# A graph layer on one core: 132 batches of gathered rows formed on TensorE in place of 128, and the node table laid out by 56 consecutive nodes to a partition

## The reference

```python
msg  = relu(x[src] + edge_attr @ We + be)
aggr = segment_sum(msg, dst, num_segments=6250)
h    = (1.0 + eps) * x + aggr
h    = relu(h @ W1 + b1) @ W2 + b2
h    = (h - mean(h, axis=0)) * rsqrt(var(h, axis=0) + 1e-5) * gamma + beta
out  = layernorm(x + relu(h) + x)
```

## Time and profile before

| | |
|---|---|
| median of 3 runs | 1557.24 us (1556.69 to 1558.63) |
| profiled execution, its own time | 1564.18 us |
| its span, first to last instruction | 1562.2 us |
| PE / PEld busy | 91% / 70% of the span |
| DVE / ACT / POOL busy | 57% / 80% / 74% |
| mean granted clock of TensorE | 0.981 |
| gathers of 128 rows | 31 out of x, 1145 out of xb, 3 for the last group |

### The profile page before, as it was taken

One profiled execution on the slowest core, in us unless ns is written; L12 is line 12 of the kernel. 1 busy time (PEld: TensorE's weight loads), 2 busy tenths in 40 slices (PEclk: granted clock), 3 DMA queues, 4 the chain that ended last, 5 costly groups with the idle time before them and its releaser, 6 DMA issues.

```text
span 1562.2 us, 60471 instructions
## 1 busy us (share of the span) xinstructions
PE 1416.0 (91%) x23435; PEld 1095.0 (70%) x23435; DVE 891.9 (57%) x3174; ACT 1255.7 (80%) x3729; POOL 1160.5 (74%) x1193
## 2 busy tenths in 40 slices
PE   1299999999999999989999999989999999999954
PEld 1277777777777777767777777767777777777734
DVE  5676665655566565555555556555556555655436
ACT  2488888888888888878877888878788888888845
POOL 7677777777777777777777777777777777777762
PEclk9999999999999999999999999999999999999967
DMA  9644445444544445444444444445444444444432
GB/s 250 170 111 109 109 113 123 113 111 117 119 113 110 108 112 126 109 106 113 111 108 106 113 106 113 112 106 117 108 110 107 111 112 107 105 112 110 104 125 84
DMA packets 148516, 180.72 MB, mean 116 GB/s; under 512 B 41725, under 2 KB 128980, under 8 KB 147972
## 3 DMA queue, kind: packets, MB, share of 16 engines
q1 hardware_dynamic: 102489, 89.62, 24.5%
q0 software_dynamic: 37728, 77.31, 20.9%
q10 hardware_dynamic: 8011, 9.90, 2.3%
HBM read 170.09 MB, written 6.63 MB: 113 GB/s over the span
## 4 chain that ended last, share of the span: by engine, by line
PE 55%; POOL 21%; issue 8%; ACT 5%; DVE 4%; DMA 4%; SPq 1%; ACTq 0%; POOLq 0%; DVEq 0%
POOL xg L590 21%; PE ps L1396 20%; PE ps L1381 14%; PE ps L1325 9%; PE ps L1311 6%; DMA xg<-xb,idxb 3%; ACT hot L747 2%; ACT msg L753 1%; PE ps L1362 1%; ACT hot L740 1%; PE ps L1342 1%; PE ps L1365 1%; PE ps L1334 1%; PE ps L1337 1%; SPq L480 1%
## 5 line engine op out<-in xcount | busy, mean ns | idle before, releaser
L590 POOL DMA_INDIRECT xg<-xb,idxb x1145 | 1107.0, 967 | 356.9 <-issue 337.0
L1396 PE MATMUL ps<-iota_all 128*128 128x128 bf16 x8064 | 518.0, 220 | 0.0
L1396 PEld LDWEIGHTS ps<-iota_all 128*128 128x128 bf16 x8064 | 452.3, 98 | 87.1 <-issue 67.7
L984 DVE TENSOR_TENSOR msg<-ps,xg 128x512 f32<-128x512 f32 x390 | 264.5, 688 | 305.6 <-DMA xg<-xb,idxb 192.8
L707 ACT ACTIVATE iota_all<-ps 128x384 bf16<-128x384 f32 x896 | 379.8, 484 | 31.7 <-PE ps L1381 28.4
L740 ACT ACTIVATE hot<-iota,rel 128x64 f32<-128x64 f32 x1560 | 391.6, 339 | 0.0
L1381 PE MATMUL ps<-x,iota_all 112*32 112x384 bf16 x7168 | 365.1, 331 | 0.0
L1069 DVE TENSOR_TENSOR accT<-accT,ps 128x64 f32 x390 | 86.2, 221 | 292.4 <-PE ps L1342 248.1
L753 ACT ACTIVATE msg<-msg 128x512 f32<-128x512 f32 x390 | 241.0, 618 | 14.7 <-DVE msg L984 14.7
L1381 PEld LDWEIGHTS ps<-x,iota_all 112*32 112x32 bf16 x7168 | 156.9, 96 | 120.6 <-issue 38.5
L1325 PE MATMUL ps<-msg,hot 128*64 128x128 f32 x3120 | 219.4, 284 | 23.1 <-ACT msg L753 23.1
(11 more groups left out here) (145 smaller groups left out, 800.3 us busy)
## 6 DMA issues: line engine op xcount, KB each, us to landing
ea<-in_eat SPq DMA_DIRECT2D x156, 320.0 KB
lowB<-lowD SPq DMA_DIRECT2D x128, 224.0 KB
xg<-xb,idxb POOLq DMA_INDIRECT x1145
accT<-in_xt ACTq DMA_DIRECT2D x1, 3125.0 KB, 14.8
x<-in_xt ACTq DMA_DIRECT2D x1, 3125.0 KB, 11.0
out<-iota_all SPq DMA_DIRECT2D x5, 512.0 KB
iota_all<-in_x ACTq DMA_DIRECT2D x3, 784.0 KB, 17.6
xb<-iota_all SPq DMA_DIRECT2D x3, 784.0 KB, 16.8
```

The lines of the kernel that those rows point to most:

```text
L590: pool.indirect_dma_start(out=xg[0:rows, slot, j, :], out_offset=None, in_=of, in_offset=bass.IndirectOffsetOnAxis(ap=index, axis=0)).then ...
L984: add = dve.tensor_tensor(both, lin_of(half), xg[:, g % RING, :, :].rearrange("p (b t) h -> p b (t h)", b=2), ALU.add)
L1396: last = pe.matmul(found[:, e, :], sel2[set_of(k)][:, t, e * P:(e + 1) * P], rows3[:, t, a, :], start=(t == 0 and e == 0 and a == 0), stop ...
```

## The change

* A batch's place in the loop is now computed: tile t of batch b is picked in visit (7b + t) * 90 // 217 - 3, and its group is three after the last of these. That is 31 batches in 90 groups where there were 30, with two or three tiles in every visit. The last batch is that of group 382, and there are 132 in all. With (7b + 6) * 90 // 217 the special groups up to 34 are 2, 5, 8, 11, 14, 17, 19, 22, 25, 28, 31, 34.
* 78 visits now have the last tiles of one batch and the first of the next. The joins of the new batch in such a visit are put later in PE's order (`parts`): behind those of the old, with `take` between them.
* `lowB` and `slotS` get a third buffer each; the 0/1 matrices remain at two sets. ACT's `take` goes ahead of `keep_slots`. The three PSUM banks of `pick` are used strictly in turn.
* Node n is now in partition n // 56, place n % 56 of `xrow` and `x3`. A partition has 56 consecutive nodes, so a piece of 14 of them is one run of 7168 bytes in HBM and in SBUF. Each load and store of a piece is cut into one transfer for partitions 0 to 95, one for 96 to 110, and for the pieces that have it one for the 34 nodes of partition 111. The bucket of an edge is its source modulo 28, its row in the bucket's table source // 28.
* The first product of a batch 0 tile now needs three of the four pieces of `x3` (before two), and four from the fourth tile on.

The core of the diff:

```diff
-    SORTED = (2, 5, 8, 11, 14, 17, 20, 23, 26, 29)
-    NB = len(SORTED)
...
+    PER, OVER = 31, 90
+    def visit_of(b, t):
+        return ((b + SKIP) * NTILE + t) * OVER // (PER * NTILE) - 3
+    def group_of(b):
+        return visit_of(b, NTILE - 1) + 3
+    NBATCH = next(b for b in range(LOOPED) if group_of(b) > 383)
...
+        def parts(i, v):
+            steps = visit(i, v)
+            cut = next((m for m, (b, t) in enumerate(steps) if t == 0 and m), len(steps))
+            return steps[:cut], steps[cut:]
...
             def keep_lifted(q):
-                sp.dma_start(xb[a * SUB:whole * SUB, :].rearrange("(b p) h -> p b h", p=SUB), xrow[0:SUB, a:whole, :])\
-                  .then_inc(s_xb[q], 16)
+                for c, d in ((0, MANY), (MANY, LASTP)):
+                    sp.dma_start(xb[c * NSUB:d * NSUB, :].rearrange("(p b) h -> p b h", b=NSUB)[:, a:b, :], xrow[c:d, a:b, :])\
+                      .then_inc(s_xb[q], 16)
+                if a < last:
+                    sp.dma_start(xb[LASTP * NSUB + a:LASTP * NSUB + last, :].rearrange("(p b) h -> p b h", p=1),
+                                 xrow[LASTP:SUB, a:last, :]).then_inc(s_xb[q], 16)
...
-                act.dma_start(xrow[0:SUB, a:whole, :], x[a * SUB:whole * SUB, :].rearrange("(b p) h -> p b h", p=SUB))\
-                   .then_inc(s_xrow[q], 16)
+                for c, d in ((0, MANY), (MANY, LASTP)):
+                    act.dma_start(xrow[c:d, a:b, :], x[c * NSUB:d * NSUB, :].rearrange("(p b) h -> p b h", b=NSUB)[:, a:b, :])\
+                       .then_inc(s_xrow[q], 16)
...
                     if not head or q:
                         window((q - 1) % STEPS, pair - 1)
-                    for j, k, t in visit(i, 2 * q):
-                        pick(j, k, t)
-                    for j, k in phase(i, q, 3):
-                        place(j, k)
-                    for j, k, t in visit(i, 2 * q - 1):
-                        join(j, k, t)
+                    for b, t in parts(i, 2 * q - 2)[1]:
+                        join(b, t)
+                    for b, t in visit(i, 2 * q):
+                        pick(b, t)
+                    for b in phase(i, q, 3):
+                        place(b)
+                    old, new = parts(i, 2 * q - 1)
+                    for b, t in old:
+                        join(b, t)
                     if not head or q:
                         turn(pair - 1)
...
-                    for j, k, t in visit(i, 2 * q + 1):
-                        pick(j, k, t)
-                    for j, k, t in visit(i, 2 * q):
-                        join(j, k, t)
-                    for j, k in phase(i, q, 4):
-                        count(j, k)
+                    for b, t in visit(i, 2 * q + 1):
+                        pick(b, t)
+                    for b, t in new:
+                        join(b, t)
+                    for b, t in parts(i, 2 * q)[0]:
+                        join(b, t)
+                    for b in phase(i, q, 4):
+                        count(b)
...
-                        x3[0:SUB, 2 * m + u, :, :].rearrange("p a h -> p (a h)"),
+                        x3[0:SUB, u * NPAIR + m, :, :].rearrange("p a h -> p (a h)"),
```

More of the change, by code:

```diff
@@ L90, in gine_layer_kernel @@
     NTILE = NPAIR // PAIRS
-    NSTEP = NB * NTILE
     VISITS = 2 * STEPS
-    FIRST = tuple(3 * k - 3 for k in range(NB))
-    SHARE = tuple((3, 2, 2) if k % 2 else (2, 3, 2) for k in range(NB))
-    K0 = 0
+    PER, OVER = 31, 90
+    SKIP = 0
     PRELUDE = 6
-    CYCLE = 3 * GROUP
-    K1 = 7
     UNBIASED = 10
@@ L102, in gine_layer_kernel, with set_of @@
     assert NPAIR == NTILE * PAIRS and CAP * PAIRS == P
[L103 to L121, removed]
+    def visit_of(b, t):
[3 more added lines that the diff above has]
+    NBATCH = next(b for b in range(LOOPED) if group_of(b) > 383)
+    BATCH_OF = {group_of(b): b for b in range(NBATCH)}
+    VISIT = {}
+    for b in range(NBATCH):
+        for t in range(NTILE):
+            VISIT.setdefault(visit_of(b, t), []).append((b, t))
+    assert len(BATCH_OF) == NBATCH and visit_of(0, 0) // 2 - 4 >= -PRELUDE
+    def set_of(b):
+        return b % 2
     FAR = 8192.0
@@ L384, in phase, with prior, at_step @@
-        def phase(i, q, ahead):
[L386 to L391, removed]
+            return i * ROUND + g in BATCH_OF
+        def prior(b):
+            return b - 2 if b >= 2 else None
+        def at_step(b, t):
+            return b * NTILE + t
@@ L393, in visit @@
+        def phase(i, q, ahead):
+            return [b for b in range(NBATCH) if visit_of(b, 0) // 2 - ahead == i * STEPS + q]
         def visit(i, v):
-            if v < 0:
-                i, v = i - 1, v + VISITS
-            return [(i + turn, k, t) for turn, k, t in VISIT[v] if live(i + turn, k)]
+            return VISIT.get(i * VISITS + v, [])
         def ending(i, v):
-            return [(j, k) for j, k, t in visit(i, v) if t == NTILE - 1]
-        def by_pool(i, g):
-            return GROUP - HALF * special(i, g)
@@ L407, in gathered @@
[L407 to L414, removed]
+            return [b for b, t in visit(i, v) if t == NTILE - 1]
+        def parts(i, v):
+            steps = visit(i, v)
+            cut = next((m for m, (b, t) in enumerate(steps) if t == 0 and m), len(steps))
+            return steps[:cut], steps[cut:]
@@ L416, in run, with by_pool, gathered @@
+        def by_pool(n):
+            return GROUP - HALF * (n in BATCH_OF)
+        def gathered(n):
+            return 16 * sum(by_pool(m) for m in range(n % RING, n + 1, RING))
         def run(eng, iteration):
@@ L602, in iteration @@
                             pool.wait_ge(s_xb[q], stores(q))
-                    if not isinstance(i, int) or i or g >= RING:
-                        wait_apart(pool, s_pre, i * ROUND + g - RING + 1)
-                    for j in range(by_pool(i, g)):
-                        gather(g % RING, j, P, idxb[h][:, at + j:at + j + 1], s_xg[g % RING], xb if biased else x)
+                    if n >= RING:
+                        wait_apart(pool, s_pre, n - RING + 1)
+                    for j in range(by_pool(n)):
+                        gather(n % RING, j, P, idxb[h][:, at + j:at + j + 1], s_xg[n % RING], xb if biased else x)
             run(pool, iteration)
@@ L1027, in ranks, with select_nodes @@
                    .then_inc(s_rel, 1)
-            def select_nodes(j, k):
-                b, old = batch(j, k), prior(j, k)
+            def select_nodes(b):
+                old = prior(b)
                 dve.wait_ge(s_lowB, 16 * (b + 1))
@@ L1342, in turn, with count @@
                 pe.transpose(ps_turned, winS[:, :], ident[:, :]).then_inc(s_turned, 1)
-            def count(j, k):
-                b = batch(j, k)
+            def count(b):
                 pe.wait_ge(s_oh, b + 1)
-                if not isinstance(b, int) or b:
+                if b:
                     pe.wait_ge(s_slotS, b)
@@ L1355, in count, with place @@
                 last.then_inc(s_cum, 1)
-            def place(j, k):
-                b, e = batch(j, k), HALF
+            def place(b):
+                e = HALF
                 pe.wait_ge(s_rank, b + 1)
```

282 lines of the change are left out of this document (134 added, 148 removed).

## The result

The changed kernel takes 1562.46 us (median of 9 runs, 1559.19 to 1564.02), the kernel before, measured beside it, 1557.8 us (9 runs, 1556.67 to 1561.32). The ratio is 1.0026, 95% interval 1.0017 to 1.0035: slower by a quarter of a per cent. Forecast were 1537 us, with a range of 1528 to 1556; the time is outside it, and the sign is wrong. The profiled execution took 1562.29 us, its span 1560.5 us, its granted clock 0.986. Two runs of kernels further down took far longer than their others, 6179.83 us (start_later_31) and 2705.11 us (both_31); they are left out of the ratios, and I have no explanation for them.

What follows compares the result with a forecast made beforehand. PE and POOL's gathers were taken to race, each bounding in turn. 14 us by the product pairs' end plus 6 in the tail made 20, so 1557.2 - 20 = 1537 us, range 1528 to 1556.

Steps and rivals of the forecast that it cites:

- The two regimes: In the loop before the change, PE sets the pace until about 630 us, then POOL's gathers at 7.61 us a pair.
- the 12 gathers: POOL's stream: four batches more mean 12 gathers fewer at 1.27 us each, 15.2 us off the stream.
- The layout: the table ahead of the loop: Ahead of the loop: runs of 7168 bytes bring the table, and with it DVE and POOL, 9 us earlier (bounds 0 and 13).
- PE's batches: PE in the loop: four batches at 6.8 us are 27 us more work, 0.15 us a pair, giving 7.20.
- these cost no instruction: New order of joins, third buffers and `take` first, in the loop: no added instruction and no added time.
- The product pairs: Pairs 143 to 182, where PE has a product more: 39 x (7.69 + 0.15) = 306 us, PE setting the pace.
- The tail: From the product pairs' end to the last group: 91.9 us before, 6 less as waits for gathers go (bounds 0 and 12).
- The baseline: The median before is 6.9 us under the profiled time; the same was taken off the forecast, 1544 to 1537 us.
- A: Rival ahead of the loop: the table is no earlier, as HBM limits many readers; 11 us less, 1546 us; chance 0.15.
- B: Rival: POOL still sets the end, PE's idle time taking its 27 us; 1529 to 1533 us; chance 0.16.
- C: Rival, slower: DVE late in 47 steps, PE's `linear` then waiting; at 0.6 us each the time is 1565; chance 0.11.
- its cover: At `place` in the loop: ranks ready 2.06 us before PE wants them, enough to hide DVE's 1.4 us delay in 47 steps.

Runs made afterwards that it cites:

- start_later_31: Changed kernel with every visit moved so that the second batch's first tile is no longer ahead of the loop; 1564.01 us, ratio 1.0044 to the kernel before.
- both_31: Changed kernel with ACT's scaling of accT behind the second batch's slots and `keep_slots` ahead of `take`; 1553.48 us, ratio 0.9966 to the kernel before.
- old_layout: Changed kernel with the node table laid out as before (node n in partition n % 112, rows of 512 bytes); 1563.52 us, ratio 1.0033 to the kernel before.
- all_31: Changed kernel, accT scaled behind the second batch's slots, `keep_slots` ahead of `take`, accT's load behind two parts of the split's second half; 1551.48 us, ratio 0.9956.
- per30: Changed kernel with 30 batches in 90 groups in place of 31, all else kept; 1556.93 us, ratio 0.9989 to the kernel before.
- slots_first_30: Changed kernel with 30 batches in 90 groups and ACT's `keep_slots` ahead of `take` again; 1555.39 us, ratio 0.999 to the kernel before.
- slots_first_31: Changed kernel, 31 batches in 90 groups kept, with ACT's `keep_slots` ahead of `take` again; 1557.5 us, ratio 0.9992 to the kernel before.
- acct_late: Changed kernel with accT's first load issued by ACT at 39 us, behind its first four table parts, not at 10.93; 1564.96 us, ratio 1.0045 to the kernel before.

## Why the prediction was wrong

Point by point, by its own steps. In spans, 1542.2 us were forecast and 1560.5 came.

**The two regimes and the 12 gathers: right.** POOL's stream has 1133 gathers from xb, its last one starts at 1499.75 (forecast near 1494, with a table 9 us earlier; that it came so near is luck, as this trace's faster gathers gave 6.6 us), and DVE's waits for gathers are gone from the loop.

**"The layout: the table ahead of the loop", 9 us: the first step that failed.** The first window stood at 87.88, not at 76: 11.9 us, the 9 us of the layout that did not come and 2.9 us by which it is later than before. I divided the engines' busy time by the megabytes, took 88 against 41 engine-us a MB for a cost of short runs, and so read a share of busy time as work. The runs showed otherwise. With runs of 7168 bytes ACT's queue kept the engines less busy (74.5% against 89.4%) and moved no more of x; old_layout and the kernel after start at 88.16 and 87.88. The stores did run faster (332 against 278 GB/s from 44 to 54 us), but up to 38 us they hardly moved: I put DVE's waits for them down to short runs, and what stood in front of them was accT's load. Before, it was issued at 25.92 and landed 14.8 us later, at 40.7. After, ACT's shorter issues (of the loads ahead of it) brought it to 10.93, and it landed 30.0 us later, at 40.9, behind the same loads of x:

```profile
accT<-in_xt ACTq DMA_DIRECT2D x1, 3125.0 KB, 30.0
```

So neither the layout nor the earlier issue moved it. all_31, which issues it behind the stores, had the last remain 7 us earlier than the kernel after (50.32 against 57.35) with the same runs; even there the first window was no earlier than in both_31, as `lowB` came late. So the step from an earlier table to an earlier first window was not shown either.

The Trainium skill, "DMA: Bandwidth & Descriptors", Specifications, gives 512 bytes as the size from which a transfer runs at line rate. I had set the trace against it; the loads of x bear the page out (the same bytes in the same time), the stores only nearly (264 and 278 against 303 to 332 GB/s). What limits the rates was not measured.

Two terms were missing in the same step. `split_sources` now works on 1170 columns where it had 390: 29.67 to 35.54 us in DVE's timeline against 29.62 to 32.11. So the last two lifts began at 35.74 in place of 32.31, with the last store and the last remain in the chain behind them. DVE's waits for stores shrank by as much, from 9.9 to 6.5 us in all, so the last remain began at 57.35 where it was at 57.26. And at 31 in 90 the second batch begins ahead of the loop: that cost the first window 5.0 us between per30 and the kernel after, 4.2 by start_later_31, 3.1 between slots_first_30 and slots_first_31. I had read the new series of groups but not asked what it puts ahead of the first window.

**PE's batches, 0.15 us a pair: too small.** It was 7.256 - 7.051 = 0.205. With the slots first, 31 and 30 in 90 differ by 7.229 - 7.051 = 0.178: that is the four batches' work, 0.03 above my 0.15. The rest, 0.027, is the step "these cost no instruction": ACT's `take` ahead of `keep_slots` makes `msg` late and a window wait. It cost 5 us in all, and 0.148 at 30 in 90, where the two meet in 63 of 64 cycles. From the first window to the first product of pair 143 it took 1126.47 - 87.88 = 1038.6 us; the forecast had 1109 - 76 = 1033, POOL's end of it, and 2 less for PE alone. The product pairs took 305.1 us, forecast 306.

**The tail: right.** From the last product to the last group 86.3 us, forecast 91.9 - 6 = 85.9, and DVE's waits for gathers there (23.6 us before, from 1430 us on) are gone.

**The baseline: the second step that failed, as far as is known.** I took the 6.9 us by which the profiled execution stood above the median off both sides. Before, the last 1100 gathers came every 1.2686 us; in per30, which has as many, every 1.2625, with the last one at 1509.1 in place of 1518.2. 1100 x 0.0061 = 6.7 us: about the whole excess lay in the stream whose waits the change removes. So it was part of the 20 us gained in that one execution, and not to be had in the median. The profiled execution after stands 0.2 us off its median. slots_first_30, with as many gathers and PE's old pace of 7.051, says the same: its pairs 75 to 143 took 508.0 us where the trace before has 514.3. That the time from gather to gather differs from trace to trace is shown (1.2625 to 1.2699 in thirteen traces, without any wait for the ring in it); that it explains the excess is argued, as the kernel before was profiled once.

The 25.5 us from 1537 to 1562.5 add up: 11.9 for the first window, 5.6 for the pairs to 143, -0.9 for the product pairs, 0.4 for the tail, 1.4 behind the last group, and 6.9 for the baseline make 25.3.

**The rivals.** A came true in its outcome, the table no earlier; its cause (what HBM gives) was not measured, and its 1546 stood on the same baseline and on a first window no later than before. B did not come: PE sets the pace everywhere. C's waits arose (41.7 us of DVE at L1027 and 42.6 at L1016, both for PE) and its cover held: PE's own waits for the ranks at `place` are four, 24.0 us in all, and all of them lie ahead of the first window. So the kernel is slower, but by another road than C.

## What to carry to other kernels

Where two streams race, the gain of shortening one ends at the other's pace, and work moved to the other is paid in all pairs, not only in those in which it is ahead: make the table by stretch for both before summing, and look for a point between (130 batches beat 128 and 132). A high busy share of DMA engines with short packets is not a reserve by itself: compare the GB/s of all queues in short stretches, and look which transfer stands in front of the one that is waited for. A profiled execution above the median has its excess somewhere, and if that is in the wait that the change removes, the gain is smaller by it.

## What the runs showed of the hardware

* Loads in rows of 512 bytes and in runs of 7168 bytes moved the same bytes in the same time (1.94 and 1.92 MB in 12 us of one queue, 213 and 211 GB/s in all), with 11 times the packets and 15 points more busy share. While the table was stored, long runs moved more: 303 to 332 GB/s from 44 to 54 us in four traces, 264 and 278 with rows of 512 bytes.
* Stores issued on SP's queue from 27 us on moved next to nothing from 30 to 38 us (0.00 and 0.07 MB) while ACT's queue carried a load of 3.2 MB; with that load issued later they moved 2.17 MB. Put later, the load held up what then came behind it: `lowB`'s 224 KB made DVE wait 5.25 us in all_31, and the last store's landing made it wait 9.28 us in acct_late.
* A load issued 15 us earlier, behind the same loads of its queue, landed at the same time (issued at 10.93 and 25.92, landed at 40.9 and 40.7).
* The time from one gather out of HBM to the next differs from trace to trace, 1.2625 to 1.2699 us as a mean over the last 1100, which is 8 us in all.
